# An attention tail rearranged in a four-layer graph network: order of ACT and DVE work, source of the last end rows, spread of a background count

## What is computed

```python
def edge_softmax(a, dst, n):
    amax = jax.ops.segment_max(a, dst, num_segments=n)
    ex = jnp.exp(a - amax[dst])
    s = jax.ops.segment_sum(ex, dst, num_segments=n)
    return ex / s[dst]
...
    k = typed_linear(x, ntype, Wk).reshape(n, H, HS)
    q = typed_linear(x, ntype, Wq).reshape(n, H, HS)
    v = typed_linear(x, ntype, Wv).reshape(n, H, HS)
    kT = jnp.einsum('nhd,htdo->nhto', k, Watt)
    vT = jnp.einsum('nhd,htdo->nhto', v, Wmsg)
    kw = kT[src, :, etype]
    m = vT[src, :, etype]
    a = jnp.einsum('ehd,ehd->eh', kw, q[dst]) * pri[:, etype].T / SQRT_D
    att = edge_softmax(a, dst, n)
    msg = (m * att[:, :, None]).reshape(-1, H * HS)
    hag = jax.ops.segment_sum(msg, dst, num_segments=n)
```

## Time and profile before

| | us |
|---|---|
| runs: median (lowest to highest of 3) | 3219.41 (3216.57 to 3222.59) |
| profiled execution, its own time | 3221.55 |
| its span, first to last instruction | 3219.7 |
| first attention's loop, 505 to 996, and its end, 996 to 1027.2 | 491.0 and 31.2 |
| first attention's tail, 1027.2 to the scatter's start at 1048.14 | 20.9 |
| second attention's loop, 1538.9 to 2030.4, and its end, to 2060.8 | 491.5 and 30.4 |
| second attention's tail, 2060.8 to the scatter's start at 2084.61 | 23.8 |

### The profile page before, as it was taken

The page is one execution under the profiler, slowest core; times in us unless marked ns, Lnnn a source line. Parts: engine busy times, 40 slices in busy tenths (PEclk is TensorE's granted clock), DMA queues, the critical chain, the costliest instruction groups (busy, mean ns, idle before and its releaser), DMA issues. The chain is left out here.

```text
span 3219.7 us, 51259 instructions
## 1 busy us (share of the span) xinstructions
PE 2404.6 (75%) x14692; PEld 1858.3 (58%) x14692; DVE 1988.7 (62%) x4492; ACT 1495.9 (46%) x3057; POOL 2005.4 (62%) x1899
## 2 busy tenths in 40 slices
PE   1678885888886266987588888533868999996887
PEld 1455664776664244665577777433655666554675
DVE  6764445777775365444577777445436888886444
ACT  0133444777775152443355555324444555554444
POOL 5457886777777755887677777673007777775000
PEclk9975667999997575556799999756888999997898
DMA  9959996777765346999699898556626666662753
GB/s 297 239 220 397 387 393 191 204 205 205 205 198 124 91 105 248 399 370 372 192 283 280 278 279 278 151 118 175 209 95 180 192 192 192 192 187 84 248 193 117
DMA packets 510362, 721.74 MB, mean 224 GB/s; under 512 B 123729, under 2 KB 393752, under 8 KB 484228
## 3 DMA queue, kind: packets, MB, share of 16 engines
q1 hardware_dynamic: 223876, 427.67, 38.5%
q0 software_dynamic: 107568, 158.76, 20.1%
q10 hardware_dynamic: 178656, 132.04, 12.8%
HBM read 334.65 MB, written 383.69 MB: 223 GB/s over the span
## 5 line engine op out<-in xcount | busy, mean ns | idle before, releaser
L1714 POOL DMA_INDIRECT att_rows<-table,kvrow x784 | 743.6, 948 | 263.9 <-issue 231.3
L2374 POOL DMA_INDIRECT msg_rows<-rows,msg_src x392 | 394.5, 1006 | 258.6 <-DMA msg_src<-in_src_pt 139.5
L1457 POOL DMA_INDIRECT matrix<-count,place x294 | 461.5, 1570 | 89.4 <-issue 89.4
L1735 PE MATMUL att_pq<-wide,att_near 128*128 x1568 | 335.2, 297 | 160.6 <-DVE att_prod L1957 93.1
L1523 DVE COPY tab_part<-tab_bank 128x512 f32<-128x512 f32 x400 | 257.5, 686 | 316.9 <-DMA table<-tab_part 274.7
L1570 PE MATMUL tab_bank<-wk,tab_kv 32*128 32x256 f32 x1600 | 336.4, 642 | 41.7 <-DVE tab_part L1523 40.2
L1735 PEld LDWEIGHTS att_pq<-wide,att_near 128*128 128x128 f32 x1568 | 252.1, 202 | 185.2 <-issue 183.5
L1542 ACT ACTIVATE tab_part<-tab_bank 128x512 f32<-128x512 f32 x400 | 217.1, 594 | 287.7 <-DMA table<-tab_part 251.1
L1737 PE MATMUL att_pq<-wide,att_far 128*128 x1568 | 317.4, 286 | 0.0
L1570 PE MATMUL tab_bank<-wv,tab_kv 32*128 32x256 f32 x1600 | 308.3, 577 | 0.0
L1570 PEld LDWEIGHTS tab_bank<-wk,tab_kv 32*128 32x128 f32 x1600 | 190.3, 282 | 139.9 <-DVE tab_part L1523 101.0
(11 more groups left out here) (464 smaller groups left out, 5516.0 us busy)
## 6 DMA issues: line engine op xcount, KB each, us to landing
table<-tab_part SPq DMA_DIRECT2D x200, 1024.0 KB
att_sums<-att_out ACTq DMA_DIRECT2D x98, 528.0 KB
gcn_cells<-matrix SPq DMA_DIRECT2D x50, 808.0 KB
att_sums<-att_out ACTq DMA_DIRECT2D x98, 272.0 KB
att_message<-in_ea_rows SPq DMA_DIRECT2D x98, 256.0 KB
msg_hidden<-hidden SPq DMA_DIRECT2D x196, 128.0 KB
sums<-msg_out ACTq DMA_DIRECT2D x98, 256.0 KB, 8.8
nb_cells<-matrix SPq DMA_DIRECT2D x25, 808.0 KB
```

Of the source, the lines that this page charges most:

```text
L1457: nc.gpsimd.indirect_dma_start(D.matrix, place, K.count[:, col:col + 1], None, compute_op=ALU.add).then_inc(added[b % BLOCKS], 16)
L1714: nc.gpsimd.indirect_dma_start(rows[g % RR][:, j, :], None, D.table, bass.IndirectOffsetOnAxis(ap=K.kvrow[:, t:t + 1], axis=0)).then_inc(r ...
L1735: nc.tensor.matmul(pq[g % 2][:, j * P:(j + 1) * P], near[g % RE][:, j, :], queries[:, bass.ds(window[j], 1), :].rearrange("p t d -> p (t d ...
L2374: nc.gpsimd.indirect_dma_start(rows[g % RR][:, j, :], None, D.rows, bass.IndirectOffsetOnAxis(ap=src[:, t:t + 1], axis=0)).then_inc(rows_i ...
```

## The change

Four things, all but the last inside `attention`.

1. In a step of ACT's loop the radial silus stand ahead of `put_out` and `keep`.
2. SP reads back only the first 95 groups' end rows from DRAM, and waits only for the stores up to group 94. The rows of groups 95, 96 and 97 go straight from the three `out` buffers to `tails`, by reads of one partition each, as soon as ACT has filled the buffer.
3. DVE does not wait for the last sum any more. The chain of maxima starts when the last messages are shared and the statistics kept; ACT's exponentials stand ahead of its copies of the end rows; DVE works out the denominators ahead of the sums; PE turns the denominators back first, ACT copies them first.
4. `COUNTS` shares the scatters out anew: 40 instead of 28 in the first projection, 36 instead of 26 in the second, 140 instead of 144 in the first table, fewer in the attentions and updates.

```diff
-COUNTS = {"qkv0": range(0, 28), "tab0": range(28, 172), "att0": range(172, 194), "upd0": range(194, 206),
-          "qkv1": range(206, 232), "tab1": range(232, 354), "att1": range(354, 376), "upd1": range(376, TILES)}
+COUNTS = {"qkv0": range(0, 40), "tab0": range(40, 180), "att0": range(180, 194), "upd0": range(194, 204),
+          "qkv1": range(204, 240), "tab1": range(240, 362), "att1": range(362, 378), "upd1": range(378, TILES)}
...
             for k in range(RO):
-                sp.wait_ge(stored[k], 16 * len(range(k, G, RO)))
-            sp.wait_ge(shared, G)
+                sp.wait_ge(stored[k], 16 * len(range(k, G - RO, RO)))
+            sp.wait_ge(shared, G - RO)
             for i in range(l + 1):
                 for j in range(J):
-                    sp.dma_start(tails[i][:, j, :, :], ends_d[i][j]).then_inc(tails_in[i], 16)
+                    sp.dma_start(tails[i][0:G - RO, j, :, :], ends_d[i][j][0:G - RO]).then_inc(tails_in[i], 16)
+            for h in range(G - RO, G):
+                sp.wait_ge(copied, copies(h + 1))
+                for i in range(l + 1):
+                    for f, p in enumerate((0, P - 1)):
+                        sp.dma_start(tails[i][h:h + 1, :, f, :], out[h % RO][p:p + 1, :, i * V:i * V + P]).then_inc(tails_in[i], 16)
+            for k in range(RO):
+                sp.wait_ge(stored[k], 16 * len(range(k, G, RO)))
...
             for i in range(l + 1):
-                pool.wait_ge(tails_in[i], 16 * J)
+                pool.wait_ge(tails_in[i], 16 * (J + 2 * RO))
             pool.wait_ge(fixed, 2 + l)
+            for k in range(RO):
+                pool.wait_ge(stored[k], 16 * len(range(k, G, RO)))
...
-                pe.wait_ge(tails_in[i], 16 * J)
+                pe.wait_ge(tails_in[i], 16 * (J + 2 * RO))
...
-            pe.wait_ge(joined, 14)
             pe.wait_ge(copied, copies(G))
-            for i in range(2 + l):
+            for i in (1, 0, 2)[:2 + l]:
+                if i == 1:
+                    pe.wait_ge(joined, 11)
+                if i == 0:
+                    pe.wait_ge(joined, 14)
...
+                for v in first_at(g):
+                    first_layer(v)
+                for v in second_at(g):
+                    second_layer(v)
                 if g >= LAG + 1:
                     put_out(g - LAG - 1)
...
-            dve.wait_ge(summed, J * G)
```

More of the change, by code:

```diff
@@ L1908, in _ @@
                         keep(c)
-                for v in first_at(g):
-                    first_layer(v)
-                for v in second_at(g):
-                    second_layer(v)
-            for i in range(l + 1):
-                for f in range(2):
-                    act.wait_ge(tipped, 2 * i + f + 1)
-                    nc.scalar.activation(edge_sum[i][:, f, :].rearrange("p (g j) -> p j g", j=J),
-                                         pq[f][:, 0:TILES].rearrange("p (j g) -> p j g", j=J), ACT.Copy).then_inc(gathered, 1)
             act.wait_ge(joined, 3)
@@ L1924, in _ @@
             nc.scalar.activation(past[:, :], past[:, :], ACT.Exp).then_inc(lifted, 1)
+            for i in range(l + 1):
+                for f in range(2):
+                    act.wait_ge(tipped, 2 * i + f + 1)
+                    nc.scalar.activation(edge_sum[i][:, f, :].rearrange("p (g j) -> p j g", j=J),
+                                         pq[f][:, 0:TILES].rearrange("p (j g) -> p j g", j=J), ACT.Copy).then_inc(gathered, 1)
             act.wait_ge(flipped, 1)
+            nc.scalar.activation(fix[:, :, P:V], po[1][0:G, 0:W:HS].rearrange("p (j n) -> p j n", j=J), ACT.Copy).then_inc(fixed, 1)
+            act.wait_ge(flipped, 2)
             nc.scalar.activation(fix[:, :, 0:P], po[0][0:G, :].rearrange("p (j d) -> p j d", j=J), ACT.Copy).then_inc(fixed, 1)
-            act.wait_ge(flipped, 2)
-            nc.scalar.activation(fix[:, :, P:V], po[1][0:G, 0:W:HS].rearrange("p (j n) -> p j n", j=J), ACT.Copy).then_inc(fixed, 1)
             if l:
@@ L2056, in _ @@
             dve.wait_ge(lifted, 2)
+            join(nc.vector.tensor_tensor(less_own, last_den, share, ALU.mult))
+            join(nc.vector.tensor_tensor_scan(run_den[:, 1:TILES + 1], decay, less_own, 0.0, ALU.mult, ALU.add))
+            dve.wait_ge(lifted, 4)
+            nc.vector.tensor_tensor(first_den, first_den, own, ALU.mult).then_inc(opened, 1)
+            nc.vector.tensor_tensor(less_own, run_den[:, 0:TILES], past, ALU.mult).then_inc(opened, 1)
+            dve.wait_ge(opened, 5)
+            join(nc.vector.tensor_tensor(first_den, first_den, less_own, ALU.add))
             dve.wait_ge(gathered, 2)
             join(nc.vector.tensor_tensor(mine, last_sum, share, ALU.mult))
-            join(nc.vector.tensor_tensor(less_own, last_den, share, ALU.mult))
             join(nc.vector.tensor_tensor_scan(run_sum[:, 1:TILES + 1], decay, mine, 0.0, ALU.mult, ALU.add))
-            join(nc.vector.tensor_tensor_scan(run_den[:, 1:TILES + 1], decay, less_own, 0.0, ALU.mult, ALU.add))
-            dve.wait_ge(lifted, 4)
-            for i, (here, run) in enumerate(((first_sum, run_sum), (first_den, run_den))):
-                nc.vector.tensor_tensor(here, here, own, ALU.mult).then_inc(opened, 1)
-                nc.vector.tensor_tensor(mine if i == 0 else less_own, run[:, 0:TILES], past, ALU.mult).then_inc(opened, 1)
-                dve.wait_ge(opened, 5 + 2 * i)
-                join(nc.vector.tensor_tensor(here, here, mine if i == 0 else less_own, ALU.add))
+            nc.vector.tensor_tensor(first_sum, first_sum, own, ALU.mult).then_inc(opened, 1)
+            nc.vector.tensor_tensor(mine, run_sum[:, 0:TILES], past, ALU.mult).then_inc(opened, 1)
+            dve.wait_ge(opened, 7)
+            join(nc.vector.tensor_tensor(first_sum, first_sum, mine, ALU.add))
             if l:
```

## The result

The changed kernel takes 3196.27 us (median of 4 runs, 3192.01 to 3197.18), the kernel before 3219.0 on the same chip; the ratio is 0.9926 (95% interval 0.9909 to 0.9943). Forecast was 3205.0 with a range from 3196 to 3213. By the ratio, 3219.41 becomes 3195.6: the sign was right, but the time came out at the range's lower edge and just outside it, with 23.8 us of gain instead of 14.4. The profiled execution took 3196.9, its span 3195.2, 24.5 us less than before.

A forecast was written before the change was run, and what follows sets the result against it. POOL's gathers were taken to pace the attention loops, PE's silu waits and a serial chain to the scatter their ends. Terms -6 - 6.1 + 0.3 - 6.0 + 3.0 + 0.4 = -14.4 gave 3205.0 us, range 3196 to 3213.

The forecast's parts named there:

- The counts: Counts shared out anew over the stages: extra ones in the projections covered by POOL's slack, +0.4 us net.
- The loop end: End of the first attention's loop: silus ahead of the evacuation cut PE's waits, -6 us (0 to -8.4).
- rival B: First attention's loop end stays as long, PE at 1.2 GHz throughout: 3210 us, up to 3213; chance 0.16.
- Behind the tips: From PE's first transpose of end rows to POOL's scatter: -6.1 us in the first attention, -6.0 in the second.
- The reads: End-row reads behind both attention loops: 95 rows get 5 DMA engines instead of 14, +0.3 and +3.0 us.
- rival A: End-row reads as quick as before, 95 rows being spread as 98 are: 3196.2 us; chance 0.12.

The follow-up runs named there:

- 96 rows: Changed kernel with the last two groups instead of three read from the output buffers, so 96 rows come from DRAM: 3189.33 us, ratio 0.9903.
- two counts: Kernel before with two counts moved from the second update to the second projection, nothing else: 3212.15 us, ratio 0.9977.
- before, and again: Kernel before the change, and the same kernel unedited, profiled once more: 3219.76 us, ratio 0.9998 for the repeat.
- order alone: Kernel before with only the new order of DVE, ACT and PE behind the attention loop, old reads, no silu move: 3203.48 us, ratio 0.9950.
- two pieces: The 96 rows kernel with its DRAM rows read as 80 early, then 16 more: 3189.38 us, ratio 0.9907.
- two queues: The 96 rows kernel with the last group's small reads issued by ACT instead of SP: 3186.46 us, ratio 0.9902.
- before with two waits: Kernel before with two already fulfilled waits added on DVE at the start of the third layer's message stage: 3214.62 us, ratio 0.9986.
- change with two waits: Changed kernel with two already fulfilled waits added on DVE at the start of the third layer's message stage: 3197.91 us, ratio 0.9939.

## Why the prediction was wrong, step by step

Two steps failed. The counts stood in the sum with +0.4, because the updates that give counts up were taken as costing nothing; the end of the second update came 3.6 us earlier. And no term stood for what two more instructions on DVE do to a later loop: the message stage came 8.0 us shorter in the two traces, 4.5 when two instructions alone were timed. The terms of the attention itself were right within 2 us.

**The loop end (-6; range 0 to -8.4).** Right in mechanism. T came 8.0 us earlier, and over the seven kernels without the silus' part T has a mean of 1026.8, over the seven with it 1018.8. PE's waits for the two silus fell from 9.7 to 3.5 us:

```profile
PE att_po_edge L1794 <- ACT att_h L1897: 3.5, 2, 1.8
```

and the row of that stretch in the table of stretches (window, us, busy by engine, clock, DMA, GB/s), against the first of the earlier trace rows:

```profile
988.00:1019.20 31.20, 23.46 (x127) 17.67 (x125) 17.91 (x43) 20.68 (x49) 25.42 (x19) 0.89 0.66 155
```

The end got shorter and the granted clock of its last 31.2 us rose from 0.78 to 0.89, so rival B, which had neither, was wrong; how much of the gain is the clock's was not separated. With the silus alone T stands at 1021.11, 6.1 us ahead of the kernel before: the forecast. The 2 us more of the whole change are not put down to one of its parts.

**Behind the tips (-6.1 and -6.0).** Right: -6.0 and -5.9, and it holds in every kernel with the order's part (8.5 and 11.2 us) but one. That one shows a condition that I had not named: had the counts of the first attention stayed at 22, half of the first gain would have been lost behind POOL (11.41 us).

**The reads (+0.3 and +3.0).** Sign and engine count right, rival A wrong although its time, 3196.2, is by luck the one that came. The packet price was fair (26.6 ns for 29.5), but the term was mis-sized at its end, by about 1 us each. In the first attention the landing behind the last data took some 1.5 us and not 0.6. In the second the big reads were through at about 2059, T + 8; what came last was SP's issue, 8.20 us for 12 small reads, 0.68 each, where I had counted nothing because the data would hide it. Some of the fit is luck: I had SP issue these reads at T - 6.2 and it did at T - 4.4, and the big reads then took less time than I had given them. 95 was a bad number, and the change lost 5 us here; 96 rows and a second queue give back 7.5. The rule cited from the Trainium skill ("DMA: Bandwidth & Descriptors", "Why a DMA increments its semaphore by 16 and not by 1") has 5 engines for 95 rows and 16 for 96; the traces agree, with 26.6% of q1 for 95 rows, under 5/16, and 55.7% for 96.

**The counts (+0.4).** Wrong. "Updates and loops give counts up" was taken as off the path without a look at the end of the second update. There the counts hold up the stores that end last, and two counts of 1.85 us less are 3.7 us. Seven kernels with 16 counts start the next stage 57.4 to 59.5 us behind the update's last gather, seven with 14 after 54.9 to 56.2. From the last gather to the message loop it is 264.3 to 268.0 and 260.7 to 263.6 us; of the -5.1 between the two traces, 3.6 lie at the update's end, and the other 1.5 are not explained.

**What no step had: the message stage, -8.0 in the traces.** The experiments put it on the place of DVE's code. A group of that loop is 12 instructions on DVE. Stretched groups come every 32 groups, 384 instructions; two instructions of shift take them away, four bring them back 11 groups earlier. That fits something that happens every 128 instructions: 128 is 10 groups and 8 instructions, so it falls on three places of the group in turn, and one of these costs POOL time. Shifted by two, it falls on three other places, and none does. The table has all kernels; its fourth column is the time from the first gather to DVE's last row of the stage:

| kernel | DVE shift | loop, us | to DVE's end, us | stretched groups begin, after the first ten |
|---|---|---|---|---|
| before, and again | 0 | 512.4, 507.7 | 531.5, 526.7 | 26, 58 (and 90) |
| counts, silus, reads, two counts, each alone | 0 | 510.9, 512.1, 508.1, 512.4 | 529.8, 531.0, 526.9, 531.2 | 26, 58 in each |
| order alone, change without counts, change | 2 | 502.4, 502.0, 502.1 | 523.8, 524.6, 523.5 | none |
| 96 rows, two pieces, two queues | 2 | 502.6, 501.5, 502.5 | 523.9, 525.5, 523.9 | none |
| before with two waits | 2 | 502.0 | 524.6 | none |
| change with two waits | 4 | 508.0 | 526.9 | 15, 47, 79 |

DVE's own rows show the event. Here are a group's product without and with it in the kernel before, and the row in which it falls after the change, again without and with it (timeline of DVE), with the row of the queue `instruction` in the stretch of each event (2537.5 to 2540 and 2519 to 2521 us):

```profile
2532.07 0.69 DVE L2485 TENSOR_TENSOR msg_prod<-msg_pr,msg_un 128x512 f32<-128x512 f32 x1 [0.36 <-PE msg_pr L2394]
...
2537.55 0.69 DVE L2485 TENSOR_TENSOR msg_prod<-msg_pr,msg_un 128x512 f32<-128x512 f32 x1 [0.71 <-PE msg_pr L2394]
```

```profile
2513.62 0.69 DVE L2512 TENSOR_TENSOR msg_vec<-msg_pm,msg_out_y 128x512 f32<-128x512 f32 x1 [0.42 <-issue]
...
2519.10 0.69 DVE L2512 TENSOR_TENSOR msg_vec<-msg_pm,msg_out_y 128x512 f32<-128x512 f32 x1 [0.77 <-issue]
```

```profile
q14 instruction: 1, 0.01, 0.8%
```

```profile
q14 instruction: 1, 0.01, 1.1%
```

Both late rows come 0.35 us later than in other groups, and both are the 64th of a block of 128 when all of DVE's rows, waits included, are counted from the program's start. Behind each of the nine 64th rows of the loop, in both traces, the queue `instruction` moves a packet within 1.7 us. In the kernel before POOL's first stretched gather starts 2.4 us behind the late row (2539.95), and in the padded changed kernel 2.4 us behind its own (2461.49 and 2463.88); after the change DVE is late in the same way and POOL keeps its step.

At each of these events POOL falls behind by about one gather, (5.49 + 5.46 + 5.69) - 3 x 5.13 = 1.25 us, and then runs on, locked at another place of the group. Once the longer gather has got to the last place, the steps stay irregular, and that is the larger loss (5.3 us a group from group 56 on in the kernel before). So the event goes with a transfer of the queue `instruction`, and a fetch of code would fit; that DVE waits for it was not tested. The Trainium skill ("Runtime: NRT & Kernel Launch", "Instruction fetch mechanics") says that code comes in blocks of 256 instructions and that crossing one is mostly hidden; here the period is 128, and the 0.35 us are not hidden at every place. Why POOL loses its step at one place and not at the others stays open.

How much of the gain this is must not be read from the loop alone. The two waits by themselves gave 0.9986, 4.5 us (interval 1.6 to 7.4), not the 6 to 10 by which the profiled loops differ, and I had expected 3208 for that kernel where it took 3214.6. The fourth column agrees with the timed value: where the gathers end early, DVE ends 21 to 24 us behind the last of them instead of 19, so that the stage takes 524.3 us on average over the seven kernels with a shift of two and 529.5 over the six with none, 5.2 less. The other parts, timed alone: silus 0.9965, order 0.9950 (with the shift in it), reads 1.0011, counts 0.9988; together 0.9914, for 0.9926 measured at once. So they add up within their intervals, which together are some 8 us wide to either side; a further cause of that size is not excluded.

## What to carry to other kernels

A change that adds a single instruction to an engine moves all code behind it on that engine, and a loop far away may change its rhythm: before a gain or a loss is put down to the idea behind a change, compare the stages that it does not touch, up to the end of the last engine in them and not of the first, and pad the kernel before by the same number of instructions. Choose the row count of a transfer for its divisors, and count its issue on the queue at the price of small reads; here 96 rows and two queues were worth 7.5 us of the tips over 95 rows and one. Work that was moved off a stage counts wherever it had been the last to end, so look at the end of each stage that gives work up, not only of those that receive it.

## What was not expected of the hardware

One-partition reads took SP 0.62 to 0.85 us each to issue (averages of a set, over the kernels that have them), against 0.43 and 0.45 for the larger reads before, and a row of reads on few engines held its issue up: eight in 6.93 us with 95 rows, in 4.53 with 96. And the place of DVE's code, by two instructions, decided between 502 and up to 512 us for the same loop, and over the whole stage between 524 and 530.
